# The layout of a bf16 one-hot tile that GpSimd writes and reads: pair-major becomes tile-major

## What is computed

```python
def _forward(x_loc, x, W1, g1, b1, W2, g2, b2, W3, g3, b3, k):
    idx = _knn(x_loc, k)                       # (8, 1024, 30) for each group of 64 channels
    pts = x_loc.transpose(0, 2, 1)
    rel = pts[bidx, idx] - pts[:, :, None, :]  # three coordinates of each neighbour, less the own
    ...
    att = jax.nn.softmax(h[..., 0], axis=-1)
    xk = x.transpose(0, 2, 1)[bidx, idx]
    agg = jnp.einsum('bnkc,bnk->bnc', xk, att)
    return x + agg.transpose(0, 2, 1)
```

## Time and profile before

| | before |
|---|---|
| median of 3 runs | 8223.11 us (8183.79 to 8232.78) |
| the profiled execution: its time | 8271.05 us |
| the profiled execution: its span | 8269.3 us |
| PE / DVE / ACT / POOL busy | 83% / 75% / 52% / 32% |
| mean granted clock of TensorE | 0.859 |
| 256 comparisons into `hm` (L561, POOL) | 398.6 us, 1709 ns each |
| 384 multiplications by `hm` (L509, POOL) | 406.1 us, 1057 ns each |
| 12 multiplications by `hm` (L1319, DVE) | 7.8 us |

### The profile page before, as it was taken

How to read it: one execution, slowest core, us unless ns; L and a number is a source line. 1 busy time by engine, 2 the same in 40 slices (tenths; PEclk the granted TensorE clock), 3 DMA queues, 4 the chain that set the end, 5 groups by cost and what they waited for, 6 DMA issues and landing times.

```text
span 8269.3 us, 204463 instructions
## 1 busy us (share of the span) xinstructions
PE 6884.4 (83%) x79422; PEld 4925.1 (60%) x79422; DVE 6179.9 (75%) x8508; ACT 4307.4 (52%) x9907; POOL 2685.8 (32%) x3399
## 2 busy tenths in 40 slices
PE   8888888888888888888888888888888759588888
PEld 5555555555555556555555555655555523488888
DVE  5777777777777777777777777777777747777777
ACT  3555555555555555555555555555555404566666
POOL 2333333333333333333333343333333310111111
PEclk9888888888888888888888888888888779899999
DMA  2111111111111111111111111111111130222222
GB/s 99 55 57 57 55 55 55 55 55 55 55 55 58 58 56 55 55 55 55 55 55 55 55 60 59 56 57 55 59 60 56 63 85 11 68 66 67 65 59 61
DMA packets 295563, 482.41 MB, mean 58 GB/s; under 512 B 103250, under 2 KB 216034, under 8 KB 293698
## 3 DMA queue, kind: packets, MB, share of 16 engines
q1 hardware_dynamic: 240205, 372.00, 15.1%
q10 hardware_dynamic: 54133, 94.55, 3.6%
HBM read 393.25 MB, written 73.25 MB: 56 GB/s over the span
## 4 chain that ended last, share of the span: by engine, by line
PE 54%; DVE 16%; ACT 15%; issue 10%; POOL 2%; DMA 1%; ACTq 1%; DVEq 0%; SPq 0%; POOLq 0%
ACT S L1047 6%; PE SCA L842 6%; PE PD L959 5%; PE SCA L811 4%; PE MISC L664 4%; PE SCA L946 3%; DVE m L1353 3%; ACT kexp L1090 3%; PE TP L834 3%; DVE pd L1359 3%; PE SCB L946 2%; PE PD L639 2%; PE SCA L682 2%; PE SCA L786 2%; PE TP L778 2%
## 5 line engine op out<-in xcount | busy, mean ns | idle before, releaser
L1353 DVE MAX8 m<-pd 128x8 f32<-128x1024 f32 x1024 | 1249.3, 1220 | 210.8 <-ACT pd L1016 99.0
L509 POOL TENSOR_TENSOR prod<-prod,hm 128x480 f32<-128x480 f32 x384 | 406.1, 1057 | 2928.8 <-ACT prod L1041 2762.2
L1357 DVE FIND_INDEX8 idx<-m,pd 128x8 uint32<-128x1024 f32 x1024 | 1248.7, 1219 | 9.5 <-issue 9.5
L1359 DVE MATCH_REPLACE8 pd<-m,pd 128x1024 f32<-128x1024 f32 x768 | 929.8, 1211 | 0.0
L639 PE MATMUL PD<-arena 128*128 128x512 f32 x1028 | 660.8, 730 | 149.7 <-ACT pd L1016 127.5
L664 PEld LDWEIGHTS MISC<-ptab,gat 128*128 128x128 bf16 x23400 | 673.8, 99 | 107.1 <-issue 77.7
L1600 DVE TENSOR_TENSOR gat<-maskT,con 120x2048 f32<-120x2048 f32 x256 | 592.1, 2352 | 171.2 <-PE SCA L946 162.3
L664 PE MATMUL MISC<-ptab,gat 128*128 128x24 bf16 x23400 | 667.5, 176 | 35.4 <-DVE gat L1309 20.6
L1047 ACT ACTIVATE S<-SCA,mx 128x64 f32<-128x64 f32 (+1 forms) x2560 | 572.0, 380 | 233.1 <-DVE mx L1365 233.1
L1365 DVE TENSOR_REDUCE mx<-SCA 128x16 f32<-128x1024 f32 (+1 forms) x192 | 235.2, 1225 | 506.9 <-PE SCA L767 456.1
L1047 ACT ACTIVATE S<-SCB,mx 128x64 f32<-128x64 f32 (+1 forms) x2560 | 570.9, 381 | 0.0
(11 more groups left out here) (270 smaller groups left out, 15192.6 us busy)
## 6 DMA issues: line engine op xcount, KB each, us to landing
gat<-low_scratch SPq DMA_DIRECT2D x396, 640.0 KB, 4.2
arena<-in_ctx ACTq DMA_DIRECT2D x33, 512.0 KB, 3.9
maskT<-in_mask ACTq DMA_DIRECT2D x32, 512.0 KB
arena<-in_x ACTq DMA_DIRECT2D x32, 512.0 KB, 6.3
x_scratch<-arena ACTq DMA_DIRECT2D x32, 512.0 KB, 4.8
x3T_scratch<-arena ACTq DMA_DIRECT2D x32, 512.0 KB, 3.7
arena<-x3T_scratch SPq DMA_DIRECT2D x32, 512.0 KB, 7.0
arena<-x_scratch SPq DMA_DIRECT2D x32, 512.0 KB, 9.3
```

The costliest lines, as they stand in the source:

```text
L1353: step(V.max(m, buf[:, :]))
L1357: last = V.max_index(idx[:, t, 8 * r:8 * r + 8], m, buf[:, :])
L1359: step(V.match_replace(buf[:, :], m, buf[:, :], -3.0e38))
```

## The change

`hm` is stored as [partition, tile, pair] where it was [partition, pair, tile]. Each comparison of L561 now writes 240 bf16 numbers that lie one behind the other, where it wrote one number in every 16 bytes. The multiplications of L509 (POOL) and L1319 (DVE) read the same numbers in the same order as before, through a view that is turned back: the eight tiles of a pair now lie 480 bytes apart, where they lay one behind the other. In both layouts each number is read three times over, for the three coordinates. Values, instructions, their number, their order on each engine, the waits and the size of the tile stay as they are.

```diff
-        hm = sb("hm", [P, NT * KNN, NT], bf16)
+        hm = sb("hm", [P, NT, NT * KNN], bf16)
...
-                done(G_.tensor_tensor(prod[:, :, :, :], prod[:, :, :, :], hm[:, pairs, :].unsqueeze(3)
-                                      .broadcast_to([P, 2 * OHROWS, NT, 3]), ALU.mult))
+                done(G_.tensor_tensor(prod[:, :, :, :], prod[:, :, :, :], hm[:, :, pairs].rearrange("p t k -> p k t")
+                                      .unsqueeze(3).broadcast_to([P, 2 * OHROWS, NT, 3]), ALU.mult))
...
-                    last = G_.tensor_scalar(hm[:, :, h], hif[:, :, :, :].rearrange("p j k a -> p (j k a)"), float(h), None,
+                    last = G_.tensor_scalar(hm[:, h, :], hif[:, :, :, :].rearrange("p j k a -> p (j k a)"), float(h), None,
                                             ALU.is_equal)
...
-                                hm[:, pairs, :].unsqueeze(3).broadcast_to([P, 2 * OHROWS, NT, 3]),
+                                hm[:, :, pairs].rearrange("p t k -> p k t").unsqueeze(3)
+                                .broadcast_to([P, 2 * OHROWS, NT, 3]),
```

## The result

| | before | changed |
|---|---|---|
| median of 11 runs | 8229.69 us (8169.52 to 8262.41) | 8297.46 us (8247.42 to 8343.64) |
| ratio | 1 | 1.0087, 95% interval 1.0054 to 1.0121 |
| the profiled execution | 8271.05 us, clock 0.859 | 8253.21 us, clock 0.867 |

A forecast was written before the change was run, and what follows sets the result against it. PE, busy for 83% of the span, was taken to bound the kernel, POOL mostly waiting. Loop 2.7 and tail 3.5 us less, multiplications 0.7 more: 8223.11 less 5.5, so 8218 us; range 8178 to 8245 us.

The forecast's parts named there:

- The comparisons: POOL's eight comparisons an item (L561) fall from 1709 to 815 ns each, 7.15 us less for each item.
- The rival that the step was not the price: Equality or bf16 output makes the 1709 ns, so L561 stays and 0.7 us are added: 8224 us; chance 7%.
- What that gives in the loop: ACT's wait at `pick(1)` for POOL goes, mostly into idle time; the loop gets 2.7 us shorter.
- the first kind of item: Ten items with a wait at `pick(1)`, where the last output transposes start 0.27 us earlier each.
- The multiplications: POOL's L509 grows by 0.045 us each from step reads, paid at 15 waits at `pick(3)`: 0.7 us more.
- The tail: After the loop, DVE's 3.48 us wait for the comparisons goes; 3.5 us less taken, 0 as the other end.
- How the numbers follow: Whole kernel: forecast 80%, rivals 20%; range 8178 to 8245 us set by how runs differ; within 1%: 94%.
- a shift of the clock that I can't work out: TensorE's clock: the reason given for allowing 3% to a kernel faster by over 1%.
- the three rivals: `pick(1)` wait paid in full, 8162 us, 5%; step not the price, 8224, 7%; step slows the multiplication, 8226, 8%.
- What would show it: Trace checks: L561 near 815 ns, L509 near 1100, ACT's L1041 wait under 20 us, 3.48 us before L1319 gone.

The follow-up runs named there:

- e2: Against the kernel before, only the comparisons changed to write in a run, with multiplications reading the old layout (wrong numbers selected): 8289.80 us, ratio 1.0039.
- e12: The changed kernel measured a third time, nothing else altered: 8291.08 us, ratio 1.0095 to the kernel before.
- the light ones: Kernel before and changed kernel, each with most terms of TensorE's heavy sums left out: 8174.13 us (old layout) and 8181.85 us (new layout).
- e11: The changed kernel plus two VectorE memsets an item, a repeat of e7 on the same chip as e12: 8156.52 us, ratio 0.9902.
- e7: The changed kernel plus two VectorE memsets in each item's first chunked attention: 8185.15 us, ratio 0.9941 to the kernel before.
- e13: The changed kernel plus two memsets on POOL, where it waits for ACT anyhow: 8280.91 us, ratio 1.0074 to the kernel before.
- e1: The changed kernel measured again, nothing else altered: 8290.79 us, ratio 1.0023 to the kernel before.

## Why the prediction was wrong, step by step

- **The comparisons: right.** 815 ns taken, 810 measured; 6.05 us less for each item where 7.15 were worked out, because the eight long ones overlapped: 12.5 us busy for 13.7 us of durations (6.4 for 6.5 with the short ones). For the same reason the group fell by 194.3 us (398.6 to 204.3) and not by the 229 of the text, which its own check, a group near 209 us, contradicts. The rival that the step was not the price is out: e2 has 808 ns with only the write side changed.
- **What that gives in the loop: right in its mechanism.** The waits at `pick(1)` are gone and reappear as waits for PE (36.5 us less, 37.2 more), and the two pairs of items above show that an item doesn't get shorter by it: 203.93 and 203.97 us, 194.91 and 194.91. The 0.27 us of the first kind of item did not show in the second pair.
- **The multiplications: too small.** 45 ns taken from L418, 114 measured in the mean and 96 between the shortest (1020 to 1116 ns). L418's 24-byte steps, read as f32 beside a second operand, were the wrong neighbour. The Trainium skill ("GPSIMD Engine Reference", section 7), with one cycle more for a read beyond 8 bytes, gave the estimates of 0.13 us for the 160 reads and 0.4 us for all 480: with 0.10 to 0.11 us the trace is near the first. The waits at `pick(3)` reached 1.1 us, at most, where they had reached 0.94; in the pictures of the first pairs that cost nothing that can be seen, in one other 0.77 us. (One slip of the sum: 2.6 us more on 1.06 is 3.5 times what a multiplication takes, not 3.6.)
- **The tail: wrong, at its other end.** The wait of 3.48 us is gone, and DVE's first multiplication comes 19.4 us after the last L541 (6593.07 less 6573.69), where it came 23.3 after. But the MLP's first matmul comes 99.9 us after it (6673.59) and came 98.0 before (6686.95 less 6588.99). Over the profiles with TensorE's full work it comes after 98.0 to 102.7 us with the long comparisons and after 98.7 to 103.0 with the short ones. No gain of 3.5 us shows; that the full DMA engines take it (share 1.04 before, 1.02 after, in a stretch at the same place) fits and isn't shown.
- **How the numbers follow: here the forecast failed.** "So the range is set by how runs differ ... I put the spread around the forecast on both sides." I took the clock as a spread of the runs that is the same for both kernels, and gave 3% to "a shift of the clock that I can't work out". This is the step that failed: the clock is not the same for both. The runs before e12 have a mean of 0.868 and e12's of 0.861, worth some 38 of the 62 us between them by the line above; of the other 24 or so the items show that part goes with where the lower level falls, and what the whole is stays open. Over all these kernels (the light ones aside), which differ by a few us of work on VectorE and by the changes on POOL and ACT, medians lie between 8157 and 8324 us. The trace had the hint: items of the kernel before come in lengths of 198 to 206 us with equal work, and I read their two kinds only for the waits of `pick(1)`. A change of this kind should have widened the range to both sides, to 8140 to 8310 us or so, with a chance near one in two for either sign (my estimate, from the medians of the runs here). None of the three rivals was this one. That the loss stayed within the 1% to which I gave 94% is luck: I put it there for another reason.
- **What would show it.** Of the checks, L561 and the wait before L1319 came as forecast, and ACT's waits for POOL nearly: 20.9 us for "under 20", with 14 waits fewer, not 18 (the 18 at `pick(1)` are gone, but there are four more at `pick(3)`). L509 (1100) and the tail did not. The last line, "the items become 1 us shorter or more with the clock as it was", asked for the right comparison and had an answer that I didn't consider: longer, with the clock not as it was.

Not settled: why a given shift leads to a given mix; theory C names no direction. No run separates the memsets' work from the place of VectorE's 0.29 us. Nor is it known what all of the 18 to 28 us are by which the changed kernel lies above the line of the clock. Nor is there a profiled execution of the changed kernel above 8300 us or of e11 near its median; that the mixes there are only more of the same is inferred from the time going with the mean clock.

## What to carry to other kernels

Where the granted clock of TensorE moves between its two levels within a loop, as here, cut the trace at one instruction of the loop and read length and granted clock of each item before costing anything: if equal work has lengths that differ by more than the change is worth, the change's own microseconds don't decide, and a forecast should be as wide as the lengths allow. Compare kernels item by item where the clock falls at the same places; that put the layout at under 0.15 us in 200 in several pictures and at 0.77 in one, where the medians said 68 us. And when a small instruction is added as a probe, look whether it moves anything besides: here it moved a stop of 0.29 us. And a version that is "slower" by under 1% in such a loop may be worth keeping and shifting: the changed kernel with two idle memsets (e11, 8156.52 us, ratio 0.9902) is the fastest one found here that leaves nothing out, but it won with the clock and would have to be tuned anew after any other edit.

## What the runs showed of the hardware

- Two memsets with 0.07 us of VectorE work an item moved the median by 105 us (e7) and 135 us (e11 against e12); one in place of two turned the sign. Two memsets on an engine with slack moved nothing that can be told (e13).
- A stop of 0.29 us at one FIND_INDEX8 of VectorE in each item changes its place with the number of instructions ahead of it (74th, 141st, 209th instruction of an item with 0, 1 and 2 memsets; none with 4, 8 and 16). What makes it isn't shown.
- The mean granted clock and the time go together over 128 runs of one kernel, 5.3 us for each 0.001; two kernels with clocks of 0.862 and 0.863 were still 31 us apart (e1).
- Taking more than a quarter of the matmuls away lowered the granted clock from 0.868 to 0.771, and gave 0.7% of time. "TensorE: Matmul & The Clock Gate" (Part 1) of the Trainium skill says that it is activity that releases the clock; that fits the direction. The same section says that the clock gate's phase at a kernel's start differs from run to run. That would fit the spread of 30 us between runs of one kernel; no run here shows that it makes it.
- On GpSimd a comparison that writes bf16 in steps of 16 bytes takes 1709 ns for 240 numbers and 810 in a run, 3.7 ns for each number. Reading in steps of 480 bytes costs the multiplication 0.6 to 0.7 ns for each of 160 jumps.
